# Orders of the last cross-attention steps and of the last stage, with low halves moved to GpSimd, in a decoder layer

## The reference

```python
x = x + self_attention(layernorm(x))              # 16 heads of 32
x = x + layernorm(rs * (cross_attention(layernorm(x), ctx, mask) @ Wo.T + bo))   # delta
xf = layernorm(x)
scores = softmax(xf @ gate_weight.T)              # 64 experts in 8 groups; 3 groups, then 6 experts a token
slot = expert * 192 + min(position_in_expert, 191)
out[e] = (silu(buf[e] @ Wg[e].T) * (buf[e] @ Wu[e].T)) @ Wd[e].T       # 64 experts, 192 slots each
x = x + sum_k(topk_w[k] * out[slot_k]) + (silu(xf @ Sg.T) * (xf @ Su.T)) @ Sd.T  # routed + shared expert
```

## Time and profile before

| | |
|---|---|
| median of three runs | 1587.62 us |
| the profiled execution | 1587.95 us |
| its span, first to last instruction | 1586.2 us |
| mean granted TensorE clock | 0.974 of full |
| TensorE busy | 1489.7 us, 94% |
| VectorE busy | 1134.6 us, 72% |
| ScalarE busy | 956.1 us, 60% |
| GpSimd busy | 711.0 us, 45% |

### The profile page before, as it was taken

The page is one execution under the profiler, slowest core; times in us unless marked ns, Lnnn a source line. Parts: engine busy times, 40 slices in busy tenths (PEclk is TensorE's granted clock), DMA queues, the critical chain, the costliest instruction groups (busy, mean ns, idle before and its releaser), DMA issues.

```text
span 1586.2 us, 30306 instructions
## 1 busy us (share of the span) xinstructions
PE 1489.7 (94%) x10344; PEld 1230.7 (78%) x10344; DVE 1134.6 (72%) x2032; ACT 956.1 (60%) x1891; POOL 711.0 (45%) x885
## 2 busy tenths in 40 slices
PE   6999998989999977869999999999999999999997
PEld 4788886778888756658888888888888888876675
DVE  5677666646888776657787777877777777755766
ACT  4566665644566454547787777777777877740120
POOL 2122234233232142245655656555556555446556
PEclk9999999999999988879999999999999999999998
DMA  6012212322221311199778877778777788357547
GB/s 206 1 61 80 68 41 74 102 89 68 69 81 46 105 50 34 47 332 356 267 261 284 281 269 259 265 266 290 270 264 270 259 283 282 128 189 235 151 159 225
DMA packets 116629, 280.25 MB, mean 177 GB/s; under 512 B 17984, under 2 KB 23104, under 8 KB 116544
## 3 DMA queue, kind: packets, MB, share of 16 engines
q1 hardware_dynamic: 98800, 228.25, 42.3%
q0 software_dynamic: 15360, 50.34, 9.8%
q10 hardware_dynamic: 2384, 0.53, 0.2%
HBM read 235.69 MB, written 43.38 MB: 176 GB/s over the span
## 4 chain that ended last, share of the span: by engine, by line
PE 47%; POOL 3%; DMA 2%; issue 2%; DVE 1%; ACT 1%; another core or an unknown queue 1%; SPq 0%; POOLq 0%; DVEq 0%
PE e_gu L2583 19%; PE e_gu L2585 9%; PE e_dn_rest L2611 5%; PE e_tr L49 3%; PE e_dn_main L41 3%; PE e_dn_main L43 3%; PE e_dn_main L42 3%; POOL h_yk L2792 2%; DMA h_yk<-y_dram,h_idx 1%; DVE h_acc L2875 1%; DMA h_xf<-xf_dram 1%; DMA e_xg<-xf_dram,e_idx 1%; PE h_gt L41 0%; PE h_up L43 0%
## 5 line engine op out<-in xcount | busy, mean ns | idle before, releaser
L2346 POOL TENSOR_TENSOR e_hid<-e_h_raw,e_hid 128x128 fp32r<-128x128 f32 (+1 forms) x192 | 166.6, 868 | 221.6 <-ACT e_hid L2411 221.6
L2583 PE MATMUL e_gu<-e_xT_hi_lo,e_wg 128*128 128x384 f32 (+1 forms) x768 | 232.1, 358 | 0.6 <-issue 0.6
L2583 PE MATMUL e_gu<-e_xT_hi_lo,e_wu 128*128 128x384 f32 (+1 forms) x768 | 230.6, 356 | 0.0
L2585 PE MATMUL e_gu<-e_xT_hi_lo,e_wu 128*128 128x192 f32 (+1 forms) x768 | 193.4, 252 | 0.0
L2585 PE MATMUL e_gu<-e_xT_hi_lo,e_wg 128*128 128x192 f32 (+1 forms) x768 | 193.2, 252 | 0.0
L2354 POOL TENSOR_TENSOR e_wd<-e_raw_d,e_wd 96x512 fp32r<-96x512 f32 x64 | 131.6, 2057 | 36.2 <-ACT e_wd L2396 36.2
L2583 PEld LDWEIGHTS e_gu<-e_xT_hi_lo,e_wg 128*128 128x128 f32 (+1 forms) x768 | 138.4, 180 | 5.8 <-issue 1.6
L2489 DVE TENSOR_TENSOR e_total<-e_gu,e_low 128x384 f32<-128x384 f32 (+1 forms) x192 | 105.6, 550 | 51.7 <-issue 44.4
L2406 ACT ACTIVATE e_low<-e_gu 128x384 f32<-128x384 f32 (+1 forms) x192 | 93.2, 485 | 80.5 <-PE e_gu L2585 73.7
L2585 PEld LDWEIGHTS e_gu<-e_xT_hi_lo,e_wg 128*128 128x128 f32 (+1 forms) x768 | 140.1, 182 | 1.4
L2583 PEld LDWEIGHTS e_gu<-e_xT_hi_lo,e_wu 128*128 128x128 f32 (+1 forms) x768 | 137.9, 180 | 3.8
(11 more groups left out here) (419 smaller groups left out, 3970.2 us busy)
## 6 DMA issues: line engine op xcount, KB each, us to landing
e_raw_g<-in_L_ffn_Wg_dram SPq DMA_DIRECT2D x64, 704.0 KB
e_raw_u<-in_L_ffn_Wu_dram SPq DMA_DIRECT2D x64, 704.0 KB
e_raw_d<-in_L_ffn_Wd_dram SPq DMA_DIRECT2D x64, 512.0 KB, 6.4
y_dram<-e_y_main SPq DMA_DIRECT2D x64, 256.0 KB, 7.8
e_raw_d<-in_L_ffn_Wd_dram SPq DMA_DIRECT2D x64, 192.0 KB, 7.5
y_dram<-e_y_rest SPq DMA_DIRECT2D x64, 128.0 KB
s_xr<-in_x_dram SPq DMA_DIRECT2D x16, 256.0 KB, 3.8
x_dram<-s_x SPq DMA_DIRECT2D x16, 256.0 KB, 2.3
```

Source lines behind the costliest of these rows:

```text
L2346: pool.tensor_tensor(hid[b][1][0:n, c, :], h_raw[g.odd][b][0:n, c, 0:P], hid[b][0][0:n, c, :].bitcast(F32), ALU.subtract).then_inc(s_hl, 1)
L2583: pe.matmul(bank[0:n, 0:2 * CAP], w[b][0][:, k, m:m + n], xT[:, :, k, toks], start=k == 0, stop=False)
L2585: ins = pe.matmul(bank[0:n, 0:CAP], w[b][1][:, k, m:m + n], xT[:, 0, k, toks], start=False, stop=k == KC - 1)
```

## The change

In the last steps of the cross-attention (`t >= 12`) and in its tail, `attn_lo` and `final_lo` leave VectorE and go to GpSimd, five and six instructions. GpSimd cannot read PSUM, so for `t >= 10` ScalarE's `final_hi` first copies the transposed row to a buffer `final_raw`, and the low half is made from that. `turn_final` stands before `project_out` in every step, the second early `shared_unit` before both, and `choose_experts` before `row_sums` in every step. The tail has a new order on all engines; one gate tile fewer (`COPIED` 3 for 4) is copied out first and passed through Silu afterwards. In the last stage `acc` has six buffers, and VectorE's `routed` pieces stand earlier.

```diff
-COPIED = 4
+AHEAD_SUMS = 6
+COPIED = 3
...
+            def attn_lo(t):                      # GpSimd
+                pool.wait_ge(s_ah, t + 2)
+                pool.wait_ge(s_pj, filled(("o", t - 1)))
+                pool.tensor_tensor(aT[1][:].rearrange("p c s -> p (c s)"), attn[:],
+                                   aT[0][:].rearrange("p c s -> p (c s)").bitcast(F32), ALU.subtract).then_inc(s_al, 1)
+            def final_lo(t):                     # GpSimd
+                pool.wait_ge(s_er[0], exchanged(0, ("xf", t)))
+                hi, lo = final_T(t)
+                pool.tensor_tensor(lo, final_raw.rearrange("p (k s) -> p k s", k=KC), hi.bitcast(F32),
+                                   ALU.subtract).then_inc(s_fl, 1)
...
                 if t >= 1:
                     residual(t - 1)
-                for i in SHARED_SPLITS.get(t - 1, ()):
+                if t >= LAST:
+                    attn_lo(t - 1)
+                units = SHARED_SPLITS.get(t - 1, ())
+                for i in units[0:2]:
+                    shared_lo(i)
+                if t >= LAST:
+                    final_lo(t - 2)
+                for i in units[2:4]:
                     shared_lo(i)
...
+                    act.activation(final_raw, ex[0][:], ACT.Copy)
+                    act.activation(final_T(t)[0], ex[0][:]..., ACT.Copy).then_inc(s_er[0], 1)
...
-                if t >= LAST:                    # VectorE
-                    row_sums(t)
                 for g in choosing:
                     choose_experts(g)
-                if t < LAST:
-                    row_sums(t)
+                row_sums(t)
...
-                if LAST > t >= 2:                # TensorE, a step
+                for i in EARLY_UNITS.get(t, ())[1:2]:
+                    shared_unit(i)
+                if t >= 2:
                     turn_final(t - 2)
                 project_out(t - 1)
-                for i in EARLY_UNITS.get(t, ())[1:2]:
-                    shared_unit(i)
-                if t >= LAST:
-                    turn_final(t - 2)
...
+            shared_unit(4)                       # TensorE, the tail
             widen(BATCH - 1)
-            shared_unit(4)
             positions(BATCH, one)
             table_part(BATCH, one - 1)
+            turn_final(BATCH - 2)
             project_out(BATCH - 1)
-            turn_final(BATCH - 2)
+            logits(BATCH - 2)
             shared_unit(5)
-            logits(BATCH - 2)
-            shared_unit(6)
             turn_final(BATCH - 1)
             logits(BATCH - 1)
+            positions(BATCH, two)
+            shared_unit(6)
             shared_unit(7)
-            positions(BATCH, two)
+            table_part(BATCH, one)
             shared_unit(8)
-            table_part(BATCH, one)
+            positions(BATCH, three)
             shared_unit(9)
-            positions(BATCH, three)
             shared_unit(10)
...
-        chunks(0, {3: (0, 0), 4: (0, 1)})        # VectorE, the last stage
-        routed(1)
+        chunks(0, {2: (0, 0), 3: (0, 1), 4: (1, 0)})
+        routed(1, late_half)
         finish(0)
         routed(2)
         finish(1)
         routed(3)
         finish(2)
         finish(3)
-        chunks(1, {1: (4, 0), 2: (4, 1), 3: (5, 0), 4: (5, 1), 5: (6, 0)})
-        routed(6, range(3, TOPK))
+        routed(4)
+        chunks(1, {0: (5, 0), 1: (5, 1), 2: (6, 0), 3: (6, 1), 4: (7, 0)})
+        routed(7, late_half)
         finish(4)
-        routed(7)
+        routed(8)
         finish(5)
+        routed(9)
         finish(6)
         finish(7)
-        chunks(2, {0: (8, 0), 1: (8, 1), 2: (9, 0), 3: (9, 1), 4: (10, 0), 5: (10, 1)})
+        routed(10)
+        chunks(2, {1: (11, 0), 2: (11, 1), 3: (12, 0), 4: (12, 1)})
         for c in range(SCN):
             hidden_lo(3, c)
         finish(8)
-        routed(11)
+        routed(13)
         finish(9)
+        routed(14)
         finish(10)
-        routed(12)
         finish(11)
-        routed(13)
-        finish(12)
-        routed(14)
-        finish(13)
         routed(15)
-        finish(14)
-        finish(15)
+        for n in range(12, BATCH):
+            finish(n)
```

More of the change, by code:

```diff
@@ L970, in cross_uses @@
             ex[0] += [("xf", t - 2), ("lg", t - 2)]
-        early = EARLY_UNITS.get(t, ())
-        proj += [("f", i) for i in early[0:1]]
+        proj += [("f", i) for i in EARLY_UNITS.get(t, ())]
         if t <= BATCH:
             proj += [("o", t - 1)]
-        proj += [("f", i) for i in early[1:2]]
         proj += units[2:3]
@@ L1374, in _ @@
             final_rstd(BATCH - 2)
+            attn_lo(BATCH - 1)
             residual(BATCH - 1)
+            final_lo(BATCH - 2)
             delta_factor(BATCH - 1)
             final_rstd(BATCH - 1)
+            final_lo(BATCH - 1)
             for c in range(SCN):
@@ L1590, in _ @@
                 shared_gate(c)
+            shared_out(6)
             shared_out(7)
[L1592 to L1595, removed]
+            table_entries(NG - 2, 0)
+            shared_out(8)
+            table_entries(NG - 2, 1)
+            shared_out(9)
+            shared_out(10)
         @block.vector
@@ L1870, in _ @@
             output(BATCH - 1)
-            final_lo(BATCH - 2)
             delta(BATCH - 1)
@@ L1874, in _ @@
             rank_experts(two)
-            final_lo(BATCH - 1)
             choose_experts(two)
@@ L2080, in _ @@
                         table_part(t, g)
-                if LAST > t >= 2:
+                for i in EARLY_UNITS.get(t, ())[1:2]:
+                    shared_unit(i)
+                if t >= 2:
                     turn_final(t - 2)
@@ L2685, in shared_programs @@
         xT = [two(sb, "xT0_", [P, KC, QT * P], F32R)]
-        unused(4 * (4 * KC * M - 2 * KC * QT * P))
+        acc = [sb(f"acc{b}", [P, H]) for b in range(3)]
         act_g = two(sb, "act_g", [P, QT * P])
         h_raw = two(sb, "h_raw", [P, QT * P])
-        acc = [sb(f"acc{b}", [P, H]) for b in range(4)]
+        acc += [sb(f"acc{b}", [P, H]) for b in range(3, AHEAD_SUMS)]
         o_sb = two(sb, "o", [P, H])
-        unused(4 * (4 * KC * M - 10 * H) - 4)
+        unused(4 * (4 * KC * M - 9 * H) - 4)
         unused(4)
@@ L2710, in shared_programs @@
         s_dn = sem("down_in_psum")
-        s_x3 = [sem(f"x3_loaded{b}") for b in range(4)]
+        s_x3 = [sem(f"x3_loaded{b}") for b in range(AHEAD_SUMS)]
         s_rh = sem("raw_hidden_loaded")
@@ L2760, in sync @@
         sp.wait_ge(*free["gate_up_of_last"])
-        for n in range(4):
+        for n in range(AHEAD_SUMS):
             load_x3(n)
@@ L2914, in vector @@
         split_lo(dve, INNER, len(pieces))
-        chunks(0, {3: (0, 0), 4: (0, 1)})
-        routed(1)
+        late_half = range(TOPK // 2, TOPK)
+        chunks(0, {2: (0, 0), 3: (0, 1), 4: (1, 0)})
+        routed(1, late_half)
         finish(0)
```

48 lines of the change are left out of this document (27 added, 21 removed).

## The result

The changed kernel takes 1566.07 us (median of 4 runs, 1562.49 to 1568.67) against 1588.33 (4 runs, 1583.06 to 1592.85): ratio 0.9866, 95% interval 0.9833 to 0.9898. That is 22 us faster where 31 were forecast, at the upper edge of the range that the forecast gave itself (1550 to 1566). A second measurement, `after_again`, gave 1564.68 and a ratio of 0.9867 (0.9826 to 0.9908).

What follows compares the result with a forecast made beforehand. The prediction saw no full engine in the cross-attention but a chain from engine to engine, and late work queued on GpSimd in the last stage. 18 + 13 = 31 us off 1587.95 gave 1557, own range 1550 to 1566.

Steps and rivals of the forecast that it cites:

- Cross-attention: Steps 12 to 15 and the tail together: the cross-attention ends 18 us earlier, bounds 12 and 22.
- step 12: Cross-attention: transposes ahead of `project_out` remove TensorE's wait of 1.96 us; gain 3 us, between 2 and 4.
- step 13: Cross-attention: the expert choice fills VectorE's wait for `sums`, so `delta(12)` begins at 580.1 for 582.79; gain 2.7 us.
- step 14: Cross-attention: early shared unit 1 goes into TensorE's idle time ahead of the low half; adds 3.7 us.
- the tail: End of cross-attention: `positions` of the middle group at 637.9 for 656.71; last shared product 16.3 us earlier, earlier gains included.
- GpSimd's part: Eleven operations moved: cost GpSimd 14.3 us, take 7.6 from VectorE; 3 us counted for slowed VectorE operations.
- Last stage: Stage after the experts: 13 us shorter, bounds 5 and 17, length about 176 for 189.60.
- (a): Last stage: rows of tile 0 added from chunk 2 on, `finish(1)` no longer waits, `down(0)` ends 3.6 us earlier.
- (b): Last stage: next `xf` rows loaded at about 1453, taking 15 us; TensorE waits until 1468, losing most of (a).
- (c): Last stage: `routed(6)` no longer ahead of the last half of `down(1)`'s input, 3.9 us gained; `hidden(2)` starts 4.9 earlier.
- (d): Last stage: gathers of tile 12 start near 1514, not 1540.47; last `finish` at 1567.2; gives 14.9 us, taken as 13.
- the last stage stays with its transfers: Rival, chance 0.15: gathers hold up the `xf` load to 1475, (c) is lost; stage gives 5 us, kernel 1565.

Runs made afterwards that it cites:

- cross_only: The changed kernel with the last stage as it was before, so only the cross-attention's part is left: 1570.8 us, ratio 0.9869.
- last_only: The kernel before with the last stage of the changed one, cross-attention as before: 1581.3 us, ratio 0.997.
- piece_release: The changed kernel, but each of a tile's six gathers waits only for the sum that last read its own sixth of the buffer: 1551.7 us.
- lows_on_vector: The changed kernel with the eleven low halves back on VectorE, without ScalarE's extra copies, new orders kept: 1563.8 us.
- mul_first: The changed kernel with the sums of tiles 4 and 10 behind the first product of hidden(1) and hidden(2): 1567.4 us.
- forced_gap: piece_release with eleven unread products on VectorE ahead of the first product of hidden(1), to force a wait on TensorE: 1561.8 us.
- vector_release: lows_on_vector with the gathers released sixth by sixth: 1559.9 us.
- piece_mul: The changed kernel with the edits of piece_release and mul_first together: 1551.1 us.
- thin_gathers: The changed kernel without three quarters of each gathered row, numbers of issues and rows unchanged: 1553.5 us.

## Why the prediction was right in direction and short in size

*Cross-attention, forecast 18, measured 19.3 in the profiles and 16.2 by `cross_only`: right.* The kernel before stood 2.84 us later already at `bounded(12)`, ahead of all that is edited; the expert stage's first instruction moved from 677.50 to 655.32, 22.2, which leaves 19.3. The profiled execution of before was on the long side here: `last_only`, with the same code, took 127.3 for 132.4. Against that one the gain is 14.3. By the steps, net of the 2.84 and with step 15 ended by `row_sums(15)`: step 12 gave 4.4 (forecast 3), step 13 2.6 (2.7), step 14 4.7 (3.7), step 15 0.8 (0.7), the tail 6.8 (9.2). `positions` of the middle group stand directly behind `logits(15)`, at 630.14 for 656.71 and so 24 us earlier net, more than the 19 to 22 forecast. What follows them took 25.2 us and not 20: shared unit 6 ran at half clock (5.3 us), as forecast, and the table parts waited for ScalarE's entries. `delta_factor` was not the releaser of `delta` in step 14. The steps' orders were not run one by one, so these shares are read from one pair of profiles. One reading of the prediction is wrong and moves nothing: VectorE's busy time in the five stretches adds up to 96.1 us, not 99.67.

*GpSimd's part, forecast near nothing: right.* Its operations took 1.26 to 1.62 us, and one wait for `c_fac` of 0.93 us is in the tail. The exclusion that "SBUF — State Buffer" of the Trainium skill describes ("Who interferes with whom"), by which I counted 8 us less if all eleven blocked, doesn't show as time. What the move cost by it and what it freed on VectorE together come to nothing that the runs can tell: 113.0 us for the cross-attention with the eleven on GpSimd, 112.4 without.

*Last stage, forecast 13, measured 1.7 in the profiles and 5.7 by `last_only`: the failing term.* By its letters:

(a) `down(0)` ends 2.9 us earlier from the stage's start (forecast 3.6).

(b) The load of the next `xf` rows, the term that I feared, cost nothing. It was issued where forecast (1433.02; less the 19.3 of the stage's start, the 1453 of the text is 1433.7). But the same load landed 11.2 us after its issue in `piece_release` and 10.5 in `lows_on_vector`, not 15, and TensorE's transposes at 1449.10 did not wait. This should have made the stage shorter than forecast.

(c) fell, and it is the step of the sum that was wrong. `hidden(2)` was to start 4.9 us earlier. Counted from the stage's start it is 2.0 later (106.4 for 104.4), since `hidden(1)` takes 6.7 more. I had moved `routed(4)` and `routed(10)` ahead of the chunks as if their rows had landed. They wait for rows, and the first product, behind them in VectorE's queue, holds TensorE's third chunk. The prediction named what is queued behind a wait for a buffer and for a bank, but not what is queued behind the wait for rows. Price in this profile: 3.06 + 1.67 us and the half clock behind. `mul_first` took both waits away and gained no time, so the profile shows this price and no run's time does.

(d) was right in kind: the gathers of tile 12 start at 1502.58, 121.4 us into the stage for 140.0 before (forecast 113.6), `down(3)` has no wait over 2 us, and the last three `finish` follow TensorE at 4.3 us each. But they follow a TensorE that is late.

The rest is late silus: 22.8 us of them in this profile. They are not all on the path. The only profile of this stage's code without them is `lows_on_vector`, 175.1 us. The prediction's 176 counts from an event 3.8 us earlier; by this cut the forecast is 185.8 less 13, or 172.8. So without late silus 10.7 of the 13 us are there. The waits before the third chunks are still in (2.87 and 1.66, with half clock behind the first); the load that did not wait makes up for part of them. The sum was nearly that of an execution without late silus, and the kernel before had fewer on its path: I took its stage for undisturbed work, and the four waits of 65.5 us that its profile puts down to "remote" for plain waiting.

The rival that came closest is "the last stage stays with its transfers" (gives 5, the kernel 1565): its number was right and its mechanism wrong, as no transpose waited for an `xf` load. The direction was earned, by the cross-attention; that the time fell at the edge of the stated range is in part luck, as the late silus could have taken more or less.

**What stays open** is why TensorE's signals come late. It isn't ScalarE, which starts 0.02 us behind them. By the runs, none of these is enough to bring it: the bytes (`piece_release` has them all and no late silu), the number and pace of GpSimd's issues (the same), a wait of TensorE ahead (`forced_gap`; in the first phase of `vector_release` there is none ahead). That one of them takes part is not excluded: without half of the gathers or with thin ones no silu was late. Instruction loading doesn't fit what is seen: the Trainium skill ("Runtime: NRT & Kernel Launch", "Instruction fetch mechanics") has instructions arrive in blocks of 16 KiB, hidden as a rule. The changed kernel's trace agrees on one instruction queue, 6 packets of 0.10 MB together in the last stage, and has smaller ones on the other, 5 of 0.04 MB; none of the 11 lands within 2 us ahead of the end of one of the three late waits shown. They come in 9 of 14 profiles, by 2 to 23 us, and `piece_release` and `piece_mul` (1549.8 to 1552.1 in 8 runs) seem to be free of them as kernels while `vector_release` (1557.6 to 1560.6) is not. Whether they hang on the build or on how the queues fall together was not settled.

## What to carry to other kernels

A sum that waits for gathered data and stands ahead of the operation that frees a bank for TensorE hands its wait on to TensorE: 3.06 and 1.67 us here, gone in `mul_first` by another order and in `piece_release` by earlier gathers. Price the landing of the data, not only the operation. Release a gather's buffer in the pieces in which it is read: one tile's six buffers released together left 29 us of pauses on the queue that everything waits for, and taking the release apart brought 14 us to the changed kernel, late silus included, 8 to the old order and 4 to `lows_on_vector`, where a new order of the whole stage had brought 5.7. Profile the same code twice before a term is read from one stage: 9 us between two kernels lay in code that both share. And before an engine is called late, look when it was signalled: here the silus were late and ScalarE was not.

## What the runs showed of the hardware

What GpSimd pays for a gather of 128 rows doesn't follow the bytes: the issue takes 0.99 us (median of 96) with rows of 512 bytes (`thin_gathers`) and 0.97 with rows of 2048 (`piece_release`), while the rows land 2.8 and 4.0 us after it, at DMA shares of 0.36 and 0.70 over the stage.

TensorE's signal of a finished chunk can be raised up to 8.1 us after the end that the profile gives the chunk's last matmul (`vector_release`, 1452.84 and 1460.92), and several signals can then come 0.06 us apart (changed kernel, 1462.16 to 1462.28). An engine that waits for it starts 0.02 us later.
